# A shared expert moved from single steps between routed blocks into the dispatch phase

## The reference, cut to what matters

```python
h2 = rmsnorm(X, norm2_w).reshape(B * S, d)
logits = h2 @ router_w
topw, topi = jax.lax.top_k(jax.nn.softmax(logits, axis=-1), TOP_K)
topw = jax.nn.softmax(topw, axis=-1)
shared = swiglu(h2, sh_gate, sh_up, sh_down)   # silu(x@gate) * (x@up) @ down
eout = ...   # the same swiglu with e_gate, e_up, e_down of each expert
spec = jnp.einsum('etd,te->td', eout, combine)
return X + (shared + spec).reshape(B, S, d)
```

## Time and profile before

| what | us |
|---|---|
| runs, median (lowest to highest) | 2482.64 (2480.54 to 2488.6) |
| the profiled execution | 2488.56 |
| its span in the trace | 2486.6 |
| busy: PE, DVE, ACT, POOL | 2029.8, 1809.3, 1667.7, 527.8 |
| `experts_stage` of layer "f", barrier to barrier | 1488.6 to 1624.0 |
| `experts_stage` of layer "h" | 2345.6 to 2480.6 |

### The profile page before, as it was taken

One profiled execution on the slowest core, in us unless ns is written; L12 is line 12 of the kernel. 1 busy time (PEld: TensorE's weight loads), 2 busy tenths in 40 slices (PEclk: granted clock), 3 DMA queues, 4 the chain that ended last, 5 costly groups with the idle time before them and its releaser, 6 DMA issues. The chain is left out here.

```text
span 2486.6 us, 44069 instructions
## 1 busy us (share of the span) xinstructions
PE 2029.8 (82%) x15480; PEld 876.2 (35%) x15480; DVE 1809.3 (73%) x4842; ACT 1667.7 (67%) x2351; POOL 527.8 (21%) x767
## 2 busy tenths in 40 slices
PE   6478598778498898898898878859898898898696
PEld 2366244556244222222222236631222222222374
DVE  7642784442775899999999735379999999995543
ACT  3133465333355499999999953435999999999443
POOL 6256310157111000000000005620000000000075
PEclk9689699789689599999999988966999999999798
DMA  3311420311420301101101021213101101100213
GB/s 69 96 39 54 86 48 3 96 37 50 92 48 3 100 16 31 31 16 31 31 16 31 2 74 37 63 37 85 31 16 31 31 16 31 30 17 2 75 47 88
DMA packets 91068, 107.79 MB, mean 43 GB/s; under 512 B 22286, under 2 KB 73700, under 8 KB 90852
## 3 DMA queue, kind: packets, MB, share of 16 engines
q1 hardware_dynamic: 78180, 83.52, 13.9%
q0 software_dynamic: 12672, 21.46, 3.2%
HBM read 73.72 MB, written 29.03 MB: 41 GB/s over the span
## 5 line engine op out<-in xcount | busy, mean ns | idle before, releaser
L1507 ACT ACTIVATE prob<-ps,score_scale 128x1024 f32<-128x1024 f32 x1024 | 1072.5, 1148 | 24.2 <-PE ps L1389 24.1
L1547 DVE TENSOR_REDUCE pair_mx<-ps 128x1 f32<-128x512 f32 x1520 | 971.9, 684 | 59.1 <-PE ps L1357 42.8
L1357 PE MATMUL ps<-k_stack,q_stack 24*128 24x512 f16 x2048 | 554.2, 403 | 63.8 <-ACT qk L1481 14.2
L1403 PE MATMUL ps<-prob,v_head 128*32 128x512 f32 x4096 | 553.8, 613 | 5.5 <-ACT prob L1507 1.2
L1389 PE MATMUL ps<-q_stack,k_stack 26*128 26x512 f16 x2048 | 389.3, 390 | 67.8 <-ACT prob L1507 64.1
L1357 PEld LDWEIGHTS ps<-k_stack,q_stack 24*128 24x128 f16 x2048 | 135.3, 92 | 474.1 <-DVE pair_mx L1547 326.3
L2423 DVE TENSOR_TENSOR hid<-silu,ps 128x256 f32<-128x256 f32 (+1 forms) x190 | 87.8, 463 | 247.3 <-PE ps L2276 168.1
L1389 PEld LDWEIGHTS ps<-q_stack,k_stack 26*128 26x128 f16 x2048 | 95.0, 91 | 400.9 <-ACT prob L1507 342.0
L1481 ACT ACTIVATE qk<-ps 128x512 f32<-128x512 f32 x264 | 164.8, 624 | 59.4 <-PE ps L1357 50.3
L1897 DVE CUSTOM_DVE_ANT_0 ps<-ps,mask 128x256 f32<-128x256 f32 (+2 forms) x512 | 179.5, 418 | 28.1 <-PE ps L1701 27.3
L2276 PE MATMUL ps<-weight_raw,block 128*128 x632 | 194.4, 431 | 0.0
(11 more groups left out here) (270 smaller groups left out, 2232.6 us busy)
## 6 DMA issues: line engine op xcount, KB each, us to landing
k_stack<-k_wide_dram SPq DMA_DIRECT2D x120, 120.0 KB
q_stack<-image_dram SPq DMA_DIRECT2D x148, 96.0 KB
arena<-e_rows SPq DMA_DIRECT2D x32, 256.0 KB, 4.9
image_dram<-parts SPq DMA_DIRECT2D x28, 128.0 KB, 3.7
weight_raw<-in_L_ffn_Wg_dram SPq DMA_DIRECT2D x6, 528.0 KB, 4.8
weight_raw<-in_L_ffn_Wu_dram SPq DMA_DIRECT2D x6, 528.0 KB, 5.1
k_stack<-image_dram SPq DMA_DIRECT2D x32, 96.0 KB
rows_in<-h_rows,gather_ids POOLq DMA_INDIRECT x158, 2.5
```

The lines of the kernel that those rows point to most:

```text
L1357: nc.tensor.matmul(max_bank(n), rows_of(c.q_stack, b, g, ROWS, slice(t * P, (t + 1) * P)), rows_of(c.k_rows, b, g, ROWS, slice(k * CHUNK, ...
L1403: ins = nc.tensor.matmul(out, c.v_head[:, e % 2, kb, :], unit, start=(kb == 0), stop=(kb == TILES - 1), skip_group_check=True)
L1507: nc.scalar.activation(c.prob[:, u % P_UNITS, :], c.ps[:, 2 * (u % 2) * CHUNK:2 * (u % 2) * CHUNK + UNIT], ACT.Exp, scale=scale).then_inc( ...
L1547: ins = nc.vector.reduce_max(mx[:, w:w + 1], max_bank(n), AX.X)
```

## The change

The shared steps are gone from the loop: `block_steps` is removed, N is the number of blocks (39), and step n is block n. Instead the shared expert is computed ahead of the router's second half, inside the dispatch phase. Its weights are stationary now and 512 tokens move, so that the hidden tile comes out transposed and needs no `turn`. TensorE runs two gate-up pairs, then `prefix`, then the other six pairs and four `down` groups, and waits for the last output before it reads the expert numbers. ScalarE copies gate (with silu) and up out of PSUM, POOL multiplies them, ScalarE copies the outputs to a new buffer `shared_sum`, and VectorE adds that to `x` in four pieces at steps 10, 14, 18 and 22. The first Exp of the router moves ahead of ScalarE's shared work. The core of the diff:

```diff
-    steps = block_steps(BLOCKS, shared)
-    step_of = {b: n for n, (kind, b) in enumerate(steps) if kind == "routed"}
-    N = len(steps)
+    N = BLOCKS
...
+    def shared_up(pe, m):
+        k, j = m // J, m % J
+        if m == 0:
+            pe.wait_ge(*shared_loaded.after(loads_of_expert(inner) * 16 + 32))
+        if m >= 2:
+            pe.wait_ge(*shared_taken.after(2 * (m - 1)))
+        for n in range(2):
+            nc.tensor.matmul(bank(c, 2 * (m % 2) + n), c.shared_raw[:, n, j * P:(j + 1) * P], c.ht[:, k * CHUNK:(k + 1) * CHUNK],
+                             start=True, stop=True).then_inc(shared_ready.sem, 1)
+
+    def shared_down(pe, k):
+        pe.wait_ge(*shared_hid.after(J * (k + 1)))
+        if k >= 2:
+            pe.wait_ge(*shared_out.after(k - 1))
+        for t in range(TPC):
+            for j in range(J):
+                ins = nc.tensor.matmul(bank(c, 4 + k % 2)[:, t * P:(t + 1) * P], c.shared_hidt[:, k % 2, j, t * P:(t + 1) * P],
+                                       c.shared_down[:, j, :], start=(j == 0), stop=(j == J - 1))
+        ins.then_inc(shared_out_ready.sem, 1)
+
+    def shared_tensor(pe):
+        for m in range(2):
+            shared_up(pe, m)
+        prefix(pe)
+        for k in range(1, CHUNKS):
+            for j in range(J):
+                shared_up(pe, k * J + j)
+            shared_down(pe, k - 1)
+        shared_down(pe, CHUNKS - 1)
+        pe.wait_ge(*shared_out.after(CHUNKS))
+
+    def shared_scalar(act):
+        def take_out(k):
+            act.wait_ge(*shared_out_ready.after(k + 1))
+            nc.scalar.activation(c.shared_sum[:, k * TPC:(k + 1) * TPC, :].rearrange("p t d -> p (t d)"), bank(c, 4 + k % 2),
+                                 ACT.Copy).then_inc(shared_out.sem, 1)
+        for m in range(J * CHUNKS):
+            if m >= 2:
+                act.wait_ge(*shared_hid.after(m - 1))
+            act.wait_ge(*shared_ready.after(2 * m + 1))
+            nc.scalar.activation(c.shared_gate[:, m % 2, :], bank(c, 2 * (m % 2)), ACT.Silu).then_inc(shared_taken.sem, 1)
+            act.wait_ge(*shared_ready.after(2 * m + 2))
+            nc.scalar.activation(c.shared_up[:, m % 2, :], bank(c, 2 * (m % 2) + 1), ACT.Copy).then_inc(shared_taken.sem, 1)
+            if m % J == J - 1 and m // J >= 2:
+                take_out(m // J - 2)
+        for k in range(CHUNKS - 2, CHUNKS):
+            take_out(k)
+
+    def shared_pool(pool):
+        for m in range(J * CHUNKS):
+            k, j = m // J, m % J
+            pool.wait_ge(*shared_taken.after(2 * (m + 1)))
+            if k >= 2:
+                pool.wait_ge(*shared_out_ready.after(k - 1))
+            pool.tensor_tensor(c.shared_hidt[:, k % 2, j, :], c.shared_gate[:, m % 2, :], c.shared_up[:, m % 2, :], ALU.mult)\
+                .then_inc(shared_hid.sem, 1)
...
+    def add_shared(dve, k):
+        tiles = slice(k * TPC, (k + 1) * TPC)
+        dve.wait_ge(*summed.after(k + 1))
+        dve.wait_ge(*shared_out.after(k + 1))
+        nc.vector.tensor_tensor(c.x[:, tiles, :], c.x[:, tiles, :], c.shared_sum[:, tiles, :], ALU.add).then_inc(shared_added.sem, 1)
...
         @block.tensor
         def _(pe):
-            prefix(pe)
+            if shared:
+                shared_tensor(pe)
+            else:
+                prefix(pe)
             pe.wait_ge(*blocks_ready.after(1))
...
         @block.scalar
         def _(act):
+            if shared:
+                probabilities(act)
+                shared_scalar(act)
             router_scalar(act)
...
+            if shared:
+                shared_pool(pool)
             pool.wait_ge(*rows_stored.after(16 * CHUNKS))
             pool.wait_ge(*ids_ready.after(2))
```

More of the change, by code:

```diff
@@ L2106, in routed_blocks @@
     return (2 * N_TOK + E * (P - 1)) // P
[L2109 to L2118, removed]
 def load_weights(sp, raw, down, weights, loaded):
@@ L2206, in experts_stage @@
     rows_stored = c.count("norm_rows_stored")
-    SUM_AT = [8 + 4 * k for k in range(CHUNKS)] if residual is not None else []
+    SUM_AT = [8 + 4 * k for k in range(CHUNKS)] if shared else []
+    ADD_AT = [10 + 4 * k for k in range(CHUNKS)] if shared else []
     results = [c.count(f"moe_results_loaded_{k}") for k in range(CHUNKS)]
@@ L2213, in routed_at @@
     def routed_at(n):
-        return steps[n][1] if n < N and steps[n][0] == "routed" else None
+        return n if n < N else None
     def turns(n):
@@ L2259, in up @@
     def up(pe, n):
[L2261 to L2268, removed]
+        pe.wait_ge(*block_ready.after(n + 1))
+        if n == 0:
+            for loaded, (first, experts) in zip(weights_loaded, expert_groups(E)):
+                pe.wait_ge(*loaded.after(experts * loads_of_expert(inner) * 16 + 32))
         if n >= 2:
@@ L2271, in up @@
         for k, ready in enumerate((gate_ready, up_ready)):
[L2272 to L2275, removed]
+            x, w = c.block[:, n % 2, :], c.weight_raw[:, bass.ds(expert[n], 1), k, :].rearrange("p o i -> p (o i)")
             nc.tensor.matmul(bank(c, 2 * (n % 2) + k, inner), x, w, start=True, stop=True).then_inc(ready.sem, 1)
     def down(pe, n):
-        kind, b = steps[n]
         pe.wait_ge(*hidt_ready.after(n + 1))
@@ L2285, in down @@
             m = sizes[j]
[L2286 to L2289, removed]
+            w = c.down[0:m, bass.ds(expert[n], 1), j, :].rearrange("p o d -> p (o d)")
             ins = nc.tensor.matmul(bank(c, 6 + n % 2, D), c.hidt[0:m, n % 2, j, :], w, start=(j == 0), stop=(j == J - 1))
@@ L2321, in silu, with probabilities @@
         nc.scalar.activation(c.silu[:, n % 2, :], bank(c, 2 * (n % 2), inner), ACT.Silu).then_inc(silu_ready.sem, 1)
+    def probabilities(act):
+        act.wait_ge(*shifted_ready.after(1))
+        nc.scalar.activation(c.probs[:, :, 0:E], c.logits[:, :, 0:E], ACT.Exp).then_inc(router_exp.sem, 1)
     def router_scalar(act):
-        if soft_of_probs:
-            act.wait_ge(*shifted_ready.after(1))
-            nc.scalar.activation(c.probs[:, :, 0:E], c.logits[:, :, 0:E], ACT.Exp).then_inc(router_exp.sem, 1)
         act.wait_ge(*shifted_ready.after(2 if soft_of_probs else 1))
@@ L2440, in add_residual @@
[L2440 to L2444 removed]
+        if n >= SCATTERS:
+            dve.wait_ge(*scattered[n % SCATTERS].after((n // SCATTERS) * 16))
+        nc.vector.tensor_copy(c.rows_out[:, n % SCATTERS], out).then_inc(out_taken.sem, 1)
+    def add_residual(dve, k):
+        tiles = slice(k * TPC, (k + 1) * TPC)
+        nc.vector.tensor_tensor(c.x[:, tiles, :], c.x[:, tiles, :], residual[:, tiles, :], ALU.add).then_inc(summed.sem, 1)
@@ L2459, in combine @@
         if SUM_AT:
-            dve.wait_ge(*summed.after(CHUNKS))
+            dve.wait_ge(*shared_added.after(CHUNKS))
         for k in range(CHUNKS):
@@ L2564, in experts_stage @@
         results[k].passed(32)
-    if SUM_AT:
-        summed.passed(CHUNKS)
+    if shared:
+        for sig in (summed, shared_out_ready, shared_out, shared_added):
+            sig.passed(CHUNKS)
+        shared_ready.passed(2 * J * CHUNKS)
+        shared_taken.passed(2 * J * CHUNKS)
+        shared_hid.passed(J * CHUNKS)
     for s, n in ((chain_s, links[0]), (weighed, 1), (scaled, CHUNKS), (rows_stored, 16 * CHUNKS), (picked, 1), (prefix_ready, 1), (blocks_ready, 1), (one_hot_ready, PIECES),
```

21 lines of the change are left out of this document (16 added, 5 removed).

## The result

| what | before | after |
|---|---|---|
| median of 4 runs, us (lowest to highest) | 2482.14 (2480.54 to 2488.6) | 2518.40 (2515.86 to 2521.96) |
| profiled execution, its span | 2488.56, 2486.6 | 2517.58, 2515.5 |
| busy PE, POOL | 2029.8, 527.8 | 2028.5, 553.9 |

The change makes the kernel 1.3% slower: the ratio is 1.013, with a 95% interval of 1.0091 to 1.0169. PE's busy time is nearly the same, so what was lost is order, not work.

The account below looks back on a forecast made before the run. POOL's gathers and scatters were taken to bound the expert loop. Per layer 19.2 us later to the first gather, less 0.9 and 0.5, is 17.8 us slower, 35.6 for two: 2482.6 + 35.6 = 2518 us, range 2499 to 2535.

Parts of the forecast that it names:

- The loop is bound by POOL, and its shared steps are nearly free: Expert loop: POOL's gather and scatter pairs, 2.57 us each, set the pace; shared steps fill time POOL leaves to PE.
- The phase on PE, 23.9 us, and on at 24.9: Dispatch: shared matmuls 13.8 + 7.1, `prefix` 1.2, half clock 1.8; PE gets on at 1513.6, the barrier ending at 1488.7.
- leave 0.3: End of the shared phase: last copy, product and hops (2.1 us) against one `down` group (1.8) leave PE 0.3 us.
- The register reads, 7.0 us: Dispatch, ahead of the slot table: PE's reads of 39 expert numbers lose their cover and cost 7.0 us.
- First gather 19.2 us later: End of the dispatch: the phase, reads and slot table put the first gather 19.2 us later per layer.
- Head gain 0.9, tail gain 0.5: Loop without shared steps: 0.9 us less before the first scatter (bounds 0 and 2), 0.5 at the last six (0 to 0.8).
- The bounds: Whole kernel: -1.4 to +3.6 us per layer around the sum, said to span 2514 to 2526 us.
- Table loads hidden: ScalarE: two added table loads of 1.28 us, under PE's work and the first gathers, cost 0, bounds 0 and 1.3.
- Rival 1, a faster POOL: Loop: without shared steps POOL's pair falls towards 1.85 us, up to 28 us per layer, 2462 in all; chance 0.05.
- Rival 2: Dispatch: the register reads aren't the 7 us, so 7.0 us per layer fall out, 2504 us; chance 0.13.
- Rival 3, half clock throughout,: Shared phase: PE stays at half clock, 20.3 us more than counted per layer, 2559 us in all; chance 0.06.
- Rival 4, half clock in the loop,: Expert loop: PE, waiting for gathers, falls to half clock for a third of blocks, 15 us per layer, 2547; chance 0.05.

Follow-up runs that it names:

- e1: The changed kernel with the shared expert left out altogether (no shared matmuls, silu, copies, products or adds): 2482.59 us, 0.9994 of the kernel before.
- e6: The changed kernel with every second gather left out in the two layers with a shared expert: 2482.85 us, 0.9978 of the kernel before.
- e9: The kernel before with every second gather left out in the two layers with a shared expert: 2477.51 us, 0.9973 of the kernel before.
- e5: The kernel before with its step order changed: routed blocks first, the 16 shared steps between blocks 5 and 37; 2486.02 us, ratio 1.0015.
- e7: The kernel before with its step order changed: shared steps after every second block from block 3 to block 33; 2487.74 us, ratio 1.0002.
- e2: The changed kernel with its 39 register reads moved into the shared phase in the shared layers: 2504.21 us, 1.0081 of the kernel before.
- e8: The changed kernel with every second gather left out in the shared layers and the register reads inside the shared phase: 2467.74 us, 0.9912 of before.
- e10: The changed kernel without POOL in the shared phase, silu writing the hidden values at once: 2517.07 us in one run, beside 2487.77 before.

## Why the prediction was right, point by point

- *The loop is bound by POOL, and its shared steps are nearly free.* Right (e1, e6): pairs 2.57 us, 0.9994 without the shared expert. What the text did not see is how thin the margin is: in the kernel before PE waits for a gather only three times in layer "f", 2.5 us in all. PE becomes the bound where POOL gets leaner (e9), and in the last blocks where PE's head start is gone (e5, e7).
- *The phase on PE, 23.9 us, and on at 24.9.* PE got on 26.6 us after the barrier (the last copy ends at 1508.39, the barrier is at 1481.81). The failed term is "leave 0.3": PE waited 1.56 us, since POOL's last two products took 4.30 us together instead of 2 x 1.26. Alone a product took 1.27 us, so that estimate held; its neighbour VectorE was left out. Half clock cost about 2.4 us (6.00 for the first eight, less 0.16, less 3.44) where 1.8 was taken, between the bounds given; `prefix` gave back 0.6, running at full clock. The last two `down` groups took 1.95 and 2.05 us where 1.78 each was taken, 0.4 more. The prediction had named a wait for POOL that makes the phase longer than 25 us as a sign of being wrong. That sign came: one term was mis-sized, while the path stayed the one that was described.
- *The register reads, 7.0 us.* Right: 1508.39 to 1515.40 in "f", 2382.46 to 2389.47 in "h", 7.01 each, and e2 takes them away.
- *The slot table, 2.35 us.* 2.24.
- *First gather 19.2 us later.* 20.8 and 20.6, mostly the 1.26 of the wait and the 0.4 of the last two groups.
- *Head gain 0.9, tail gain 0.5.* 1.9 and about 0. The head was sized from layer "b", whose wider rows hide that the three first steps cost nearly 2 us; e1 without them needs 10.6 and 10.4 us. It lies inside its bounds of 0 to 2, and cancels part of what the gather was out by: 18.5 to 18.9 net where 17.8 was said, so 37.3 over both layers instead of 35.6. That the number is out by only 0.4 us is luck: errors of 1.3 to 1.6 us and of 1.0 us per layer had opposite signs, and the medians lie 36.3 apart.
- *The bounds.* From -1.4 to +3.6 us per layer the sum spans 2515 to 2525, where 2514 to 2526 stands; nothing hangs on it.
- *Table loads hidden.* From the barrier of layer "f" to the first silu of its loop there are now three loads where there was one. The first stands at 1483.65 and its silu follows at 1484.94, 0.01 us after its 1.28 us. The second, 1508.41 to 1509.69, is done long before its Exp, which waits for VectorE until 1520.66. The third, 1524.86 to 1526.14, has its silu at 1526.15; it is the one that runs under the first gathers, as the only load did before, and the prediction took it for the second. The first multiplication of the loop follows at 1526.57, 0.2 us after PE's matmuls for it end. By the rule in the Trainium skill, "ScalarE: Activation LUTs", section "What ACT_TABLE_LOAD costs", a drain of 1.38 us would come on top; no such time is seen: ScalarE's work ahead of each load ends 0.02 us before it, and behind the first and the third the silu starts at once.
- *Rival 1, a faster POOL*, falls with the pairs of 2.57. *Rival 2* falls with e2. *Rival 3, half clock throughout,* falls with PEclk 1.00 in the windows from 1488 to 1505. *Rival 4, half clock in the loop,* falls with PEclk 1.00 at 1540 to 1560, although PE waits for a gather in most blocks: 25 times from 1531 to 1612 us, 15.8 us in all, the longest 1.5. The loop in the section "HAM oscillation" of the Trainium skill's "TensorE: Matmul & The Clock Gate" waits longer for each DMA than it computes; here the waits are the shorter part, so its rule doesn't reach this loop, and the trace agrees.

## What to carry to other kernels

Before moving work off an engine that is busy all the time, ask which engine's rows show no waits but its own issue gaps: here POOL's were like that, and all of the other engine's filler could be left out for 0.2% at most. A phase with an idle engine is only free for as long as that idle time lasts, and what hides behind another engine's work (here 39 register reads, 7 us) comes out as soon as the order changes; put such reads between long groups of matmuls. The same move can pay on a kernel whose indirect DMAs are fewer: with half the gathers e6 is level with e9, and e8, with its reads hidden, is 10 us ahead. That would need a loop with fewer POOL instructions that still computes everything, which wasn't tried, and no version measured here that computes everything beats the kernel before.

## What the runs showed of the hardware that was not expected

POOL and VectorE hold each other up. Beside POOL's products, two short operations of VectorE end when the product does. After, layer "f", POOL and then VectorE (timelines):

```profile
1490.91 1.27 POOL L2491 TENSOR_TENSOR shared_hidt<-shared_gate,shared_up 128x512 f32<-128x512 f32 x1 [1.16 <-ACT shared_up L2478]
1492.63 1.26 POOL L2491 TENSOR_TENSOR shared_hidt<-shared_gate,shared_up 128x512 f32<-128x512 f32 x1 [0.45 <-ACT shared_up L2478]
...
1497.85 2.25 POOL L2491 TENSOR_TENSOR shared_hidt<-shared_gate,shared_up 128x512 f32<-128x512 f32 x1 [0.19 <-ACT shared_up L2478]
1501.35 4.30 POOL L2491 TENSOR_TENSOR shared_hidt<-shared_gate,shared_up 128x512 f32<-128x512 f32 x2 [1.25 <-ACT shared_up L2478]
```

```profile
1491.12 1.09 DVE L2354 TENSOR_SCALAR block_expert<-block_of 128x39 int32<-128x39 f32 x1
...
1493.04 0.90 DVE L2359 CAST place_i<-place 128x32 int32<-128x32 f32 x1
```

`block_expert` ends at 1492.21 and the product at 1492.18; the cast ends at 1493.94 and the next product at 1493.89. Both take 0.18 us with POOL idle (e10: 0.18 for each). Not every operation is held: a TENSOR_REDUCE of 128x256 beside the second product takes 0.42 us (1492.58 to 1493.00), as in e10, and the product keeps its 1.26. The other way round, a product takes 2.25 us, and two take 4.30, beside the one-hot work. The Trainium skill has this in "SBUF — State Buffer", section "Who interferes with whom": the two engines share a pair of ports, VectorE needs it for some forms of copy, cast and tensor_scalar and for operations with two inputs in SBUF, and whoever comes first holds it for the whole instruction. The trace agrees for these operations, and e10 puts a price on it: 3.21 us of the one-hot row (7.83 against 4.62), which nothing waits for here. The other price is most of PE's wait of 1.56 us, which is on the way to the first gather in each layer: about 1.3 us by an estimate, since the last copy of `up` ended at 1503.00 and a product of 1.27 us behind it would have ended at 1504.3 instead of 1505.65.
